# A block of two feed-forward stages and an attention: in half of the attention's steps the score unit is issued in front of the maxima unit

## The reference, cut to what matters

```
x = x + 0.5 * ffn(layernorm(x))      # silu(x w1) * (x w2), gelu(. h1), gelu(. h2), . w3
x = x + attn(layernorm(x))           # q k^T * 8**-0.5, softmax, v, Wo
x = x + 0.5 * ffn(layernorm(x))
```

## Time and profile before

| | us |
|---|---|
| median of 3 timed runs | 623.59 |
| their range | 621.62 to 624.64 |
| the profiled execution's own time | 617.05 |
| its span, first to last instruction | 615.2 |
| TensorE busy in the span | 589.1 (96%) |
| ScalarE, VectorE busy | 466.4 (76%), 443.6 (72%) |
| mean granted clock of TensorE | 0.99 of full |

### The profile page before, as it was taken

One profiled execution on the slowest core, in us unless ns is written; L12 is line 12 of the kernel. 1 busy time (PEld: TensorE's weight loads), 2 busy tenths in 40 slices (PEclk: granted clock), 3 DMA queues, 4 the chain that ended last, 5 costly groups with the idle time before them and its releaser, 6 DMA issues.

```text
span 615.2 us, 12580 instructions
## 1 busy us (share of the span) xinstructions
PE 589.1 (96%) x4452; PEld 439.3 (71%) x4452; DVE 443.6 (72%) x1000; ACT 466.4 (76%) x796; POOL 98.3 (16%) x262
## 2 busy tenths in 40 slices
PE   2999999999999999999999999999989999999996
PEld 2788788788686766565656565766678878788785
DVE  7995855868558778798988897885665756855742
ACT  4677977968865578788787878877877977968964
POOL 2092020022021103132231302102020020020000
PEclk9999999999999799999999999999999999999999
DMA  8300000000074306171625343400000001000011
GB/s 282 86 2 1 0 2 1 0 0 1 1 273 145 130 2 220 56 255 62 235 89 187 137 139 142 134 2 1 2 1 1 1 1 36 0 26 8 1 34 37
DMA packets 36693, 42.02 MB, mean 68 GB/s; under 512 B 2464, under 2 KB 27296, under 8 KB 36640
## 3 DMA queue, kind: packets, MB, share of 16 engines
q1 hardware_dynamic: 36640, 41.31, 19.8%
HBM read 22.42 MB, written 18.87 MB: 67 GB/s over the span
## 4 chain that ended last, share of the span: by engine, by line
PE 73%; ACT 9%; DVE 8%; issue 5%; DMA 3%; SPq 1%; POOL 0%; ACTq 0%; DVEq 0%; POOLq 0%
PE bank L1092 39%; PE bank L1204 9%; PE bank L1179 8%; PE bank L1191 4%; PE bank L1193 3%; DVE silu L842 3%; DVE act_lo L833 2%; ACT silu L544 2%; DVE neg_max L883 2%; PE bank L1161 1%; PE bank L1222 1%; PE bank L1169 1%; ACT act_hi L536 1%; ACT act_hi L559 1%; DMA QK<-qk_scratch 1%
## 5 line engine op out<-in xcount | busy, mean ns | idle before, releaser
L1092 PE MATMUL bank<-act_hi,WH 128*128 128x512 f32 x576 | 230.5, 400 | 3.8 <-ACT act_hi L559 1.5
L1092 PE MATMUL bank<-act_lo,WH 128*128 128x512 f32 x576 | 225.7, 392 | 0.0
L883 DVE TENSOR_REDUCE neg_max<-bank 128x2 f32<-128x512 f32 x256 | 166.8, 681 | 32.6 <-PE bank L1179 30.4
L678 ACT ACTIVATE probs<-bank 128x512 f32<-128x512 f32 x256 | 139.3, 598 | 38.6 <-PE bank L1193 37.0
L853 DVE TENSOR_TENSOR act_lo<-full,act_hi 128x512 fp32r<-128x512 f32 x128 | 91.5, 719 | 101.7 <-ACT act_hi L559 101.4
L557 ACT ACTIVATE full<-bank,SG 128x512 f32<-128x512 f32 x128 | 88.1, 688 | 65.8 <-PE bank L1092 65.0
L1092 PEld LDWEIGHTS bank<-act_hi,WH 128*128 128x128 f32 x576 | 108.2, 188 | 31.2 <-ACT act_hi L559 4.7
L1092 PEld LDWEIGHTS bank<-act_lo,WH 128*128 128x128 f32 x576 | 108.3, 188 | 23.1 <-issue 1.0
L1191 PE MATMUL bank<-QK 32*128 32x256 f32 x512 | 96.1, 334 | 0.4 <-ACT probs L678 0.4
L559 ACT ACTIVATE act_hi<-bank,SG 128x512 fp32r<-128x512 f32 x128 | 87.1, 681 | 0.0
L1193 PE MATMUL bank<-m_parts,SEL 32*128 32x256 f32 x512 | 82.1, 280 | 0.0
(11 more groups left out here) (94 smaller groups left out, 570.7 us busy)
## 6 DMA issues: line engine op xcount, KB each, us to landing
qk_scratch<-qk SPq DMA_DIRECT2D x64, 256.0 KB, 2.6
QK<-qk_scratch SPq DMA_DIRECT2D x16, 1024.0 KB, 7.6
raw_rest<-w_ffn SPq DMA_DIRECT2D x4, 512.0 KB, 5.8
out<-X SPq DMA_DIRECT2D x4, 512.0 KB, 3.2
X<-x SPq DMA_DIRECT2D x3, 512.0 KB, 7.7
raw<-w_ffn SPq DMA_DIRECT2D x3, 256.0 KB, 4.5
X<-x SPq DMA_DIRECT2D x2, 256.0 KB, 3.2
WA<-w_att SPq DMA_DIRECT2D x1, 256.0 KB, 5.6
```

What stands on the lines that cost most here:

```text
L678: A.activation(probs[:, v % 8, :], bank[B_BANKS[bb][v]][:, :], ACT.Exp, scale=SCALE)\
L883: D.tensor_reduce(neg_max[:, bb, qt, n0:n0 + 2], bank[(banks or A_BANKS[bb])[u]][:, :].rearrange("p (h k) -> p h k", h=2), axis=AX.X, op=A ...
L1092: ins = MM(dst, a, b, start=k == 0, stop=k == len(todo) - 1)
```

## The change

In steps 0 and 1 of every four the score unit now stands in front of the maxima unit; in steps 2 and 3 the order stays. The products with V still come behind both units, and the transpose of the maxima behind step 1. In the first batch the waits for `m_lo` and `x_added` belong to the score unit of step 4 and so move in front of that step's maxima unit. Only the order within TensorE's list changes.

```diff
-                    if more:
+                    scores_first = u % 4 < 2
+                    if more and not scores_first:
                         max_scores(b + 1, npar, nbb, u, A_BANKS[nbb], A_BANKS[bb] if prev else ENTRY_BANKS)
-                    for d, v in in_step(u, prev, own):
-                        at = (b - d, par, bb) if d == 0 else (b - d, ppar, pbb)
-                        if d == 0 and v == 0:
+                    units = [(v, (b - d, par, bb) if d == 0 else (b - d, ppar, pbb)) for d, v in in_step(u, prev, own)]
+                    for v, at in units:
+                        if at[0] == b and v == 0:
                             pe.wait_ge(m_lo, b + 1)
                             if not prev:
                                 pe.wait_ge(x_added, NB + CREDIT)
                         if v < UNITS:
                             scores(*at, v)
-                        if d == in_step(u, prev, own)[-1][0] and u == 1 and own:
-                            rows_of_max()
+                    if more and scores_first:
+                        max_scores(b + 1, npar, nbb, u, A_BANKS[nbb], A_BANKS[bb] if prev else ENTRY_BANKS)
+                    if u == 1 and own and prev:
+                        rows_of_max()
+                    for v, at in units:
                         if v >= 7 and v % 4 == 3:
                             weigh(*at, v // 4 - 1, 0)
                             weigh(*at, v // 4 - 1, 1)
```

## The result

Over 21 timed runs of each kernel the changed one took 623.72 us at the median (619.88 to 629.85), the one before 619.39 (615.66 to 625.68; the three runs shown earlier were slower than most of these). The ratio is 1.0062, 95% interval 1.0036 to 1.0089: **slower by 0.6%**, where the forecast said 1.0 us less and within 0.5%.

A forecast was written before the change was run, and what follows sets the result against it. Pace was set by step 0's score unit, its exponential, step 3's score unit and the product with V. Gains of 0.6 (bursts) and 0.4 (first batch) made 623.59 - 1.0 = 622.6 us, range 619.9 to 625.3.

The forecast's parts named there:

- The maxima units, later. I cost this at nothing.: In the swapped bursts: first reduction 0.01 to 0.02 us later, absorbed by slack before step 3's score unit; cost nothing.
- cover: In step 3 of a four: the maxima unit is ready 0.21 us before the score unit behind it.
- the waits in front of the outer transposes stay where they were: Steps 3, 7, 9 and 13: the swap leaves these waits in place; no cost counted.
- The rule weighed against the trace: The skill's rule that matmuls start and end in program order; judged contradicted by the trace, kept as a small-chance rival.
- single file: Rival on TensorE: units run one matmul after another, maxima 0.48 us later, 0.27 us lost per four; 639.5 us; chance 5%.
- The swap inside a burst: In 59 bursts: score units start 0.01 us sooner, gaining 0.6 us in all, bounds 0 to 1.8.
- The first batch: Step 4: score units start before the maxima's wait, projection of V 0.43 us sooner; 0.4 us gain taken, bounds 0 to 0.6.
- The slow clock stretch: Rival: TensorE's half-clock stretch from 207.2 to 217.4 us goes away, 2.7 us more gain, 619.9 us; chance 10%.

The follow-up runs named there:

- the added matmul: One redundant matmul added to step 0's score unit: on the changed kernel 162.68 us steady part, ratio 1.0295; on the kernel before 158.90 us, ratio 1.0170.
- with the loss taken out of the way: VectorE's reductions halved (half of the keys left out): new order 151.94 us steady part, ratio 0.9908; old order 152.19 us, ratio 0.9961.
- step 1 alone: Against the kernel before, score unit first only in step 1 of every four: steady part 153.43 us, ratio 0.9976.
- step 3 alone: Against the kernel before, score unit first only in step 3 of every four: steady part 153.39 us, ratio 0.9988.
- the first batch alone: Against the kernel before, the new order only in the first batch, the old one in all others: steady part 153.43 us, ratio 1.0008.
- step 2 alone: Against the kernel before, score unit first only in step 2 of every four: steady part 154.46 us, ratio 1.0053.

## Why the prediction was wrong

**The step that failed is "The maxima units, later. I cost this at nothing."** It let the first reduction start later by 0.01 to 0.02 us, the delay of the unit's start, and kept 0.19 of 0.21 us of cover. The reduction came 0.27 us later (0.54 to 0.81), because the signal that VectorE waits for is now given only behind that of the score unit of step 0 in front. The cover was overrun by 0.27 - 0.21 = 0.06 us in the four of the earlier trace rows, and 0.05 us was lost there (1.51 to 1.56). Over all fours the loss is 0.079 on average. Part of the fours had less cover than the one that I read: in batch 2 the score unit of step 15 started 1.42 us behind its burst (244.29 to 245.71), not 1.51, since ScalarE took up the exponential 0.31 us behind the last score matmul (244.75 to 245.06) and not 0.38 (302.63 to 303.01), and under the new order it too went at 1.56. I had read the cover from one four and used it for 59. Told apart by fours, a four of batches 4 to 11 loses 0.05 to 0.07 us and one of batches 12 to 14 loses 0.12 to 0.16, with two exceptions: steps 8 to 11 of batches 4 to 12, which have a projection between their bursts, lose nothing, and steps 4 to 7 of batches 5, 7 and 9, with the transpose that waits for VectorE's residual, lose 0.27. That second way I had not followed at all: "the waits in front of the outer transposes stay where they were" is true of the order, not of the time at which VectorE gets there.

**The rule weighed against the trace.** I discarded it whole for being wrong in half. The Trainium skill, "TensorE: Matmul & The Clock Gate", section "The mechanism" in the part on packing small matmuls, says that matmuls start and end in program order. The starts here do not the earlier trace rows; the signals, which is what other engines live by, do, as the semaphore increments and the added matmul show. The matmul ends in the trace are modelled, and I had taken them for the moment of the signal. The trace of before could have told me: its maxima unit of step 1 stands behind the longer score unit of step 0, and was signalled 0.277 us behind its recorded end in the median (302.681 to 302.955 in batch 6), against 0.014 for that of step 0. The views that I read don't print the signals, and no start showed it, since VectorE came to that unit later still.

**The rival "single file"** had the right place and the right point of decision (0.21 us), with a delay of 0.48 in place of the measured 0.27, so 0.27 us per four in place of 0.08, and 5% of the chance. A version of it with starts as traced and signals in order would have read: score unit's last matmul at 0.46 instead of the maxima unit's at 0.22, 0.24 later, 0.03 beyond the cover; 1.8 us over 59 fours from this one four, and more with the fours of less cover.

**The swap inside a burst**: right in sign. The gain was 0.6 us by forecast; with the loss taken out of the way 0.006 per four was measured, 0.3 us over 59. (The before kernel and those with step 1 alone, step 3 alone or the first batch alone changed lie within 0.04 us of each other in the steady part, so the 0.25 us is more than such scatter.)

**The first batch**: the projection of V came 0.43 us sooner as worked out, of which 0.29 was kept (forecast 0.4).

**The slow clock stretch**: its chance was 10%. It was shorter in the one profile of the changed kernel, but not with the same order in the first batch alone, and as short (3.41 us) in that of "step 2 alone", which keeps the old order in steps 4 and 5. The runs spread over nearly the same mean clocks, 0.977 to 0.996 before and 0.976 to 0.997 after. That the order has no influence on it at all is not shown.

**The sum after the fact**: 59 x 0.079 = 4.7 us of loss, less 0.29 in the first batch, is 4.4; at nearly equal clock 4.1 was timed. The profiled pair shows 2.83: the first batch, with its shorter slow stretch, gave back 2.43 (15.62 us from the first maxima unit to batch 1, then 13.19), batches 1 to 14 cost 4.29 (196.81, then 201.10), and what stands before and behind them cost 0.65 and 0.31.

## What to carry to other kernels

When work for two engines runs side by side on TensorE, put the short unit first, and read when its consumer started, not when the trace says the matmul ended. A swap that leaves every start where it was can still move every signal; what decides is the slack of whoever waits behind that signal, and it has to be read in each kind of repetition, not in one.

## What the runs showed of the hardware

- Matmuls of units in different row groups started out of program order (in the changed kernel a maxima unit at 301.87, ahead of the older score unit's last at 302.32), but their signals came in program order, 476 of 476 in each of twelve kernels, at least 0.042 us apart. Nothing older unfinished, a unit was signalled 0.014 us behind its last matmul's recorded end; behind a longer unit that started 0.01 us earlier, 0.278.
- At the consumer: in three kernels the reduction started 0.35 us behind the start of the older unit's last matmul (302.32 to 302.67, 318.38 to 318.73, 297.60 to 297.95), and 0.33 to 0.34 (0.31 in the median of batches 4 to 13) behind its own last matmul where nothing older was unfinished.
- Dispatch past a busy row group ends somewhere: with four matmuls ahead in one row group the next unit started 0.01 us behind it, with five 0.23 us, just behind the start of the second of the five (318.02, then 318.03). In the old order the longer unit held back the second maxima unit in the same way (309.00, then 309.23). Whether it is the number that decides, or something else about the added matmul, which writes where the next one writes, no run here parts.
